# Two key chunks' weighted sums in one visit, two visits a step instead of four, with a fourth buffer of probabilities

## The reference

```python
x = x + attention(layernorm(x), ctx, ctx, k_length)
#   attn = softmax(SCALE * log(k_length) * einsum('bhdq,bhdk->bhqk', qh, kh))
#   out  = einsum('bhqk,bhdk->bhdq', attn, vh)
x = x + moe(layernorm(x), Wg, w1, w2)     # 8 experts, the best 2 of each row, capacity 1280
```

## Time and profile before

| | |
|---|---|
| runs (3) | median 2185.14 us, 2181.98 to 2186.24 |
| profiled execution | 2179.5 us, its span 2177.8 us |
| TensorE busy | 2117.0 us, 97% |
| VectorE busy | 1008.1 us, 46% |
| ScalarE busy | 712.9 us, 33% |
| attention stage, tail, experts | to 615 us, to 677 us, to the end |

### The profile page before, as it was taken

How to read it: one execution, slowest core, us unless ns; L and a number is a source line. 1 busy time by engine, 2 the same in 40 slices (tenths; PEclk the granted TensorE clock), 3 DMA queues, 4 the chain that set the end, 5 groups by cost and what they waited for, 6 DMA issues and landing times. The chain is left out here.

```text
span 2177.8 us, 27085 instructions
## 1 busy us (share of the span) xinstructions
PE 2117.0 (97%) x10179; PEld 1518.8 (70%) x10179; DVE 1008.1 (46%) x1908; ACT 712.9 (33%) x1216; POOL 470.4 (22%) x593
## 2 busy tenths in 40 slices
PE   3999999999999999999999999999999999999997
PEld 1445454455547888878888887888888788888776
DVE  5677878878765434234324423423432342343211
ACT  1666666666652222113212212311311231132110
POOL 3334444343422111110301201031030102101101
PEclk9999999999999999999999999999999999999999
DMA  9876767776635435212613612422441252241101
GB/s 147 160 165 157 181 157 188 168 187 162 146 114 161 115 70 132 58 22 85 131 20 78 150 26 58 125 50 43 114 98 25 56 134 52 48 125 31 16 6 20
DMA packets 183895, 216.61 MB, mean 99 GB/s; under 512 B 39731, under 2 KB 111419, under 8 KB 183740
## 3 DMA queue, kind: packets, MB, share of 16 engines
q1 hardware_dynamic: 154128, 173.21, 34.1%
q0 software_dynamic: 22240, 37.92, 9.1%
q10 hardware_dynamic: 7372, 3.42, 0.7%
HBM read 113.93 MB, written 68.29 MB: 84 GB/s over the span
## 5 line engine op out<-in xcount | busy, mean ns | idle before, releaser
L1590 DVE SCALAR_TENSOR_TENSOR hlo<-ps_h,hhi 128x512 fp32r<-128x512 f32 x256 | 177.0, 692 | 928.4 <-ACT hhi L1467 928.4
L1467 ACT ACTIVATE hhi<-ps_h 128x512 fp32r<-128x512 f32 x256 | 152.9, 597 | 1123.4 <-PE ps_h L1731 1123.4
L1729 PE MATMUL ps_h<-xhi,w1hi 128*128 128x512 f32 x1024 | 404.9, 395 | 2.5 <-PEq L1316 1.3
L1748 PE MATMUL ps_y<-w2hi,hhi 128*128 128x512 f32 x1024 | 404.7, 395 | 0.7 <-DVE hlo L1590 0.7
L1749 PE MATMUL ps_y<-w2lo,hhi 128*128 128x512 f32 x1024 | 403.0, 394 | 1.0 <-issue 1.0
L1750 PE MATMUL ps_y<-w2hi,hlo 128*128 128x512 f32 x1024 | 403.7, 394 | 0.0
L1731 PE MATMUL ps_h<-xhi,w1lo 128*128 128x512 f32 x1024 | 403.6, 394 | 0.0
L1730 PE MATMUL ps_h<-xlo,w1hi 128*128 128x512 f32 x1024 | 403.0, 394 | 0.0
L678 DVE TENSOR_REDUCE nmax<-ps_s 128x1 f32<-128x512 f32 x512 | 335.7, 681 | 128.5 <-PE ps_s L1086 124.6
L460 ACT ACTIVATE probs<-ps_t 128x512 f32<-128x512 f32 x504 | 273.0, 604 | 183.1 <-PE ps_t L1037 145.8
L1729 PEld LDWEIGHTS ps_h<-xhi,w1hi 128*128 128x128 f32 x1024 | 192.3, 188 | 48.5 <-issue 3.9
(11 more groups left out here) (202 smaller groups left out, 2007.2 us busy)
## 6 DMA issues: line engine op xcount, KB each, us to landing
raw<-in_L_ffn_w SPq DMA_DIRECT2D x128, 512.0 KB, 4.9
qst<-qhi SPq DMA_DIRECT2D x64, 256.0 KB, 5.8
xin<-dispatched SPq DMA_DIRECT2D x60, 256.0 KB, 5.8
kst<-khi SPq DMA_DIRECT2D x52, 256.0 KB, 6.4
xt<-in_x SPq DMA_DIRECT2D x32, 256.0 KB, 3.1
ct<-in_ctx SPq DMA_DIRECT2D x32, 256.0 KB, 4.5
qst<-qlo SPq DMA_DIRECT2D x32, 256.0 KB, 6.8
xres<-in_x SPq DMA_DIRECT2D x32, 256.0 KB, 4.7
```

The source lines that it names most:

```text
L1467: nc.scalar.activation(hhi[k % 2][:], ps_h[k % 3][:], ACT.Relu).then_inc(hhi_ready, 1)
L1590: nc.vector.scalar_tensor_tensor(hlo[k % 2][:], ps_h[k % 3][:], 0.0, hhi[k % 2][:].bitcast(F32), ALU.max, ALU.subtract).then_inc(h_ready, 1)
L1729: nc.tensor.matmul(to, w1hi[:, c, fs], xhi[n % 2][:, c, :], start=(c == 0), stop=False)
L1748: nc.tensor.matmul(ps_y[b][:], hhi[k % 2][:, bs], w2hi[:, f, :], start=(f == 0), stop=False)
```

## The change

A step has two visits, each with two chunks: after chunk 0's pairs the sums of chunks 2 and 3 of group s - 3, after chunk 2's pairs those of chunks 0 and 1 of group s - 2. probs gets a fourth buffer, and an exponential waits for the sums four chunks back instead of three. To make room, the small tensor spare_over shares the memory of x2t. The tail is rearranged in the same way, with a single call for chunk 2 of the last group ahead of the last sums.

```diff
--- before.py
+++ after.py
@@ -131,7 +131,6 @@
         spare_i = sb("spare_i", [P, E, FILLS], I32)
         spare_0 = sb("spare_0", [P, E, FILLS])
         spare_f = sb("spare_f", [P, E, FILLS])
-        spare_over = sb("spare_over", [P, E, FILLS])
         totals_f = sb("totals_f", [P, E])
 
         xt = [sb(f"xt{i}", [P, D]) for i in range(4)]
@@ -139,7 +138,7 @@
         ct = [sb(f"ct{i}", [P, D]) for i in range(4)]
         qst = [sb(f"qst{i}", [P, HPG, D], F32R) for i in range(KR)]
         kst = [xin[:, :, 0:D] if i == XIN_AT else sb(f"kst{i}", [P, HPG, D], F32R) for i in range(KR)]
-        probs = [sb(f"probs{i}", [P, HPG, D]) for i in range(3)]
+        probs = [sb(f"probs{i}", [P, HPG, D]) for i in range(4)]
         vt = [sb(f"vt{i}", [P, NC4, P]) for i in range(4)]
         qf = sb("qf", [P, D])
         qhi = [sb(f"qhi{i}", [P, D], F32R) for i in range(2)]
@@ -162,6 +161,7 @@
         st2 = [sb(f"st2_{i}", [P, 12]) for i in range(2)]
         xrow = sb("xrow", [P, RING, ROW])
         x2t = sb("x2t", [P, D])
+        spare_over = x2t[:, 0:E * FILLS].rearrange("p (e n) -> p e n", e=E)
 
         lg = [sb(f"lg{i}", [P, 2, E]) for i in range(2)]
         lmax = sb("lmax", [P, 2])
@@ -455,9 +455,9 @@
                 n = NC4 * g + c
                 k = t_turn["t", g, c, i]
                 act.wait_ge(t_done, k)
-                if i == 0 and n >= 3:
-                    act.wait_ge(pv_done, n - 2)
-                nc.scalar.activation(probs[n % 3][:, i, :], t_at(k)[:], ACT.Exp).then_inc(t_free, 1)
+                if i == 0 and n >= 4:
+                    act.wait_ge(pv_done, n - 3)
+                nc.scalar.activation(probs[n % 4][:, i, :], t_at(k)[:], ACT.Exp).then_inc(t_free, 1)
 
             def values(g):
                 k = t_turn["vt", g]
@@ -961,10 +961,10 @@
             nc.vector.tensor_tensor(spare_f[:], spare_0[:], bcast(totals_f[:], [P, E, FILLS]), ALU.add
                                     ).then_inc(spare_ready, 1)
             dve.wait_ge(spare_ready, 1)
-            nc.vector.tensor_tensor(spare_over[:], spare_f[:], bcast(e_cap[:], [P, E, FILLS]), ALU.is_ge
+            nc.vector.tensor_tensor(spare_over, spare_f[:], bcast(e_cap[:], [P, E, FILLS]), ALU.is_ge
                                     ).then_inc(spare_ready, 1)
             dve.wait_ge(spare_ready, 2)
-            nc.vector.scalar_tensor_tensor(spare_f[:], spare_over[:], float(1 << 20), spare_f[:], ALU.mult, ALU.add
+            nc.vector.scalar_tensor_tensor(spare_f[:], spare_over, float(1 << 20), spare_f[:], ALU.mult, ALU.add
                                            ).then_inc(spare_ready, 1)
             dve.wait_ge(spare_ready, 3)
             nc.vector.tensor_copy(spare[:], spare_f[:].rearrange("p e n -> p (e n)")).then_inc(spare_ready, 1)
@@ -1004,19 +1004,19 @@
                         pe.wait_ge(o_saved, g)
                 for h in range(HPG):
                     hd = slice(HD * h, HD * h + HD)
-                    nc.tensor.matmul(ps_o[hd, :], vt[g % 4][:, c, hd], probs[n % 3][:, h, :],
+                    nc.tensor.matmul(ps_o[hd, :], vt[g % 4][:, c, hd], probs[n % 4][:, h, :],
                                      start=(c == 0), stop=(c == NC4 - 1))
                 if c == 0 and g >= 1:
                     pe.wait_ge(l_saved, g)
                 for h in range(HPG):
                     hd = slice(HD * h, HD * h + HD)
-                    done = nc.tensor.matmul(ps_l[hd, :], ones[:, 0:HD], probs[n % 3][:, h, :],
+                    done = nc.tensor.matmul(ps_l[hd, :], ones[:, 0:HD], probs[n % 4][:, h, :],
                                             start=(c == 0), stop=(c == NC4 - 1))
                 done.then_inc(pv_done, 1)
 
             def last_weighted():
                 pe.wait_ge(t_free, t_turn["t", G - 1, NC4 - 1, HPG - 1])
-                held = probs[(4 * G - 1) % 3]
+                held = probs[(4 * G - 1) % 4]
                 for h in range(HPG):
                     hd = slice(HD * h, HD * h + HD)
                     done = nc.tensor.matmul(ps_l[hd, :], ones[:, 0:HD], held[:, h, :], start=False, stop=True)
@@ -1112,9 +1112,11 @@
                         if i == 1 and c == 1 and live(s - 4):
                             shares(s - 4)
                     if c == 0 and live(s - 3):
-                        weighted(s - 3, NC4 - 1)
-                    if c > 0 and live(s - 2):
-                        weighted(s - 2, c - 1)
+                        weighted(s - 3, 2)
+                        weighted(s - 3, 3)
+                    if c == 2 and live(s - 2):
+                        weighted(s - 2, 0)
+                        weighted(s - 2, 1)
 
             def warm(n):
                 for _ in range(n):
@@ -1127,7 +1129,12 @@
                     turned_logits(g, c, 1)
                     if g == G - 2 and c == 0:
                         shares(G - 4)
-                    weighted(g if c else g - 1, (c - 1) % NC4)
+                    if c == 0:
+                        weighted(g - 1, 2)
+                        weighted(g - 1, 3)
+                    if c == 2:
+                        weighted(g, 0)
+                        weighted(g, 1)
                     if c == 0:
                         row_turned(g - 3)
                     if g == G - 2:
@@ -1149,6 +1156,7 @@
                             places(B - 1, 0, 2)
                     turned_logits(g, c, 2)
                     turned_logits(g, c, 3)
+            weighted(G - 1, 2)
             last_weighted()
             row_turned(G - 2)
             pe.wait_ge(dve_const, 4)
```

## The result

| | before | changed |
|---|---|---|
| runs (4 each), median | 2183.56 us | 2216.53 us |
| lowest to highest | 2180.17 to 2186.24 | 2214.93 to 2225.94 |
| profiled execution, its span | 2179.5, 2177.8 us | 2215.12, 2213.4 us |
| ratio, 95% interval | | 1.0163, [1.0138, 1.0188] |

The change costs 33 us. The forecast was +17, with a range that ended at 2215.

The account below looks back on a forecast made before the run. TensorE was taken as the bound, with its readers falling behind in runs of pairs. 14.5 x 1.24 = +18.0 us and the tail's -1.0 gave +17, so 2185.14 would become 2202 us; range 2181 to 2215.

Parts of the forecast that it names:

- What bounds the kernel: Attention stage: TensorE bounds on average, busy 38.87 of 38.97 us; readers fall behind in runs of pairs, catch up in visits.
- A dropped visit gives 0.28 us: TensorE time saved per merged visit: 0.09 shorter added chunk, 0.09 at entry, 0.10 exposed weight load.
- V0 to V2: From visit after chunk 0 to visit after chunk 2, pairs unbroken: +0.39 us in odd, +0.46 in even steps.
- the two chains named: Chunks 1 to 2: ScalarE's copies, exponentials and khi hold vt; VectorE's product into o_sb holds chunk 2's first scores.
- V2 to V0: From visit after chunk 2 to next step's after chunk 0: +0.29 us even into odd, +0.10 odd into even.
- The sum over two steps: Attention loop, one odd and one even step: 0.39 + 0.46 + 0.29 + 0.10 = +1.24 us, taken 14.5 times.
- The tail: Last two groups, without score matmuls: four waits go (-1.9), chunk 2's sums add +0.9; net -1.0 us, bounds -2.5 and +1.8.
- What would show it: Signs in the changed trace: two steps 40.2 us instead of 38.97, double visit 3.63, TensorE waiting for o_sb and probs.
- rival 1: The forecast itself: stalls outweigh the visits' cost, +17 us, from +12 to +30; chance 0.68.
- the second: Rival: readers keep up and only the 0.28 us per dropped visit remains, -16 us, 2169; chance 0.13.
- the third: Rival: they cancel, readers stalling TensorE only from V2 to V0; 2181.6, up to 2189.5 us; chance 0.15.
- The fourth: Rival: a worse wait, for instance VectorE not drained in the longer visit, debts carrying over; about 2217 us; chance 0.04.

Follow-up runs that it names:

- The merges: Two kernels with one double visit a step instead of the changed kernel's two: sums of chunks 0 and 1, or of 2 and 3; 2195.48 and 2198.94 us.
- the light readers: Changed kernel and kernel before, each with maxima and exponentials over 256 of 512 columns; only the attention stage read: two steps 36.9 and 36.8 us.
- khi_early: Changed kernel with ScalarE's khi moved from after chunk 1 to before the copies of ps_o and ps_l: 2224.41 us, 1.0189.
- self_wait: Changed kernel with VectorE's wait for its own last maximum of a step moved to GpSimd: 2199.37 us, 1.0079.
- four_self: Kernel before, four visits, with VectorE's wait for its own last maximum of a step moved to GpSimd: 2185.45 us, 0.9997.
- wait_long: Kernel before, with TensorE's fourth score matmul of chunk 0 in each step waiting for the maximum just before it: 2257.55 us, 1.0344.
- wait_short: Kernel before, with TensorE's fourth score matmul of chunk 0 in each step waiting for the maximum two turns back, not three: 2191.38 us, 1.0050.

## Why the prediction was right in sign and too small

- **What bounds the kernel** was right: TensorE bounds it, and the visits are the time in which the readers catch up. The merges and the light readers show it (1.73 us of difference in two steps with full readers, 0.1 to 0.2 with light ones).
- **A dropped visit gives 0.28 us**: right to 0.06. The double visit took 3.57 us, 0.06 under the forecast, and a half step in which nothing waits is 0.31 to 0.34 shorter. In the kernels that were run this saving never reached the total.
- **V0 to V2, +0.39 and +0.46**: measured +0.42 and +0.48, by the two chains named. TensorE waits for "ACT probs" before vt and for "DVE o_sb" at c = 2, as forecast, and khi_early, which shortens the first chain, takes 0.5 us out of the even step's V0 to V2.
- **V2 to V0, +0.29 and +0.10**: this step of the working failed; it measured +0.46 and +0.37. "VectorE's last two maxima of c = 3 start at 424.75 and 425.35, the next, now with its scores there, at 425.95" takes the next maximum to follow 0.60 behind. The code has a wait in between, 0.3 us, which no row shown of before tells, because V3 lay over it. It was to be read in the code, not in the trace. self_wait and four_self measured it: without the wait odd into even is 0.04 us above before, and even into odd 0.12, both under the forecast. That 0.29 for even into odd was near 0.46 at all owes something to chance: the forecast had it all from the chain through r_rows and qhi, and without VectorE's wait only 0.12 is left.
- **The sum over two steps, +1.24** became +1.73, so 28 steps gave 23.6 us instead of 18.0.
- **A term was missing**, the largest part of the error: TensorE's clock. The prediction takes the granted clock of the earlier trace rows (1.00) for all steps and adds the new waits at their own length. Five stretches at 1.2 GHz came with them, which cost 9.9 us, over half of the 18.6 us by which the forecast (17.0) fell short of the profiled difference (35.6). wait_long shows that waits of 1.4 us and more bring such stretches with four visits too; wait_short shows that 27 waits of 0.2 to 0.3 us bring none there. Why single waits of 0.28 us are followed by falls in the changed kernel stays open.
- **The tail, -1.0**: +2.2, a little beyond the upper bound of +1.8. Three stretches of 3.4 us at 1.2 GHz more than before lie between the loop and the experts; I didn't separate them from its own waits. Why the tail lost is open.
- **What would show it** named 40.2 us for two steps, from the earlier trace rows. That was a slip: the window of 38.97 us there is longer than two steps, which are 37.60 from V2 to V2. The sum of the prediction didn't use it. The low end of rival 1 is a slip too: with r_rows issued in 1.14 the sum of two steps is 1.24 - 0.50 = 0.74, not 1.00, so +8 and not +12. The stated range doesn't use it.
- **The rivals**: the second (only the drain, -16) and the third (they cancel) are out, since no merge gained and V0 to V2 lost what was read. The fourth (2217) had the time but not the cause: VectorE isn't in debt for a whole microsecond; it waits for itself for 0.3, and the clock adds its part. That its number fits is luck. The Trainium skill, TensorEngine Tiling (Array Packing), Key Properties, has the drain; its size here is in the rows (0.31 to 0.34 us for a dropped visit, with the exposed load), and it was outweighed in each place where a reader used the visit.

## What to carry to other kernels

Work of the bounding engine that asks nothing of its readers is cover for them, so before such pieces are merged, list what each one hides, from the code as well as from the trace: a wait under cover leaves no row. Waits of TensorE cost more than the idle time that the profile lists (0.5 us for 0.24 in wait_short), and more still when the clock falls behind them; add up the granted clock's stretches when a sum of waits doesn't reach the measured time. And when an edit on one engine lets another start earlier, look there too: holding GpSimd back was worth 30 us in one kernel here.

## What the runs showed of the hardware

- The granted clock fell for 3.4 or 6.8 us at a time in the middle of the attention stage, where TensorE was busy for 482.73 of 500 us (changed kernel, 100 to 600 us). Behind 24 waits of 1.4 to 2.3 us it fell 19 times (wait_long), behind 27 waits of 0.2 to 0.3 us never (wait_short), but behind single waits of 0.27 to 0.29 us three times in the changed kernel. A fall of 3.4 us made its step 1.4 to 2.1 us longer, and 2.2 to 2.8 together with waits beside it.
- One small VectorE operation doubled its time with the new order: one row of the groups from 300 to 600 us of the kernel before (busy us, mean ns),

```profile
L746 DVE TENSOR_TENSOR hot<-e_f,topi 128x32 f32<-128x32 f32 x8 | 4.2, 521 | 0.0
```

and the same of the changed kernel:

```profile
L746 DVE TENSOR_TENSOR hot<-e_f,topi 128x32 f32<-128x32 f32 x8 | 9.1, 1137 | 0.0
```

In both kernels it ends within 0.06 us of the end of GpSimd's residual (L336, 1.27 us), in all cases but one. With the new order it starts when that one has just begun, and so lasts as long; the changed kernel's timeline:

```profile
317.98 1.29 POOL L336 TENSOR_TENSOR x<-o_sb,xres 128x512 f32<-128x512 f32 x1
...
318.04 1.27 DVE L746 TENSOR_TENSOR hot<-e_f,topi 128x32 f32<-128x32 f32 x1
```
